# Cross attention and routed FFN on one core: block weights copied to fixed places by SyncE, half of the first normalisation on ScalarE

## The reference

```
c = layernorm(x)
s = (c @ w_c + b_c) + (q @ w_q + b_q)^T + (c * w_cq) @ q^T + b_cq      # 1024 x 6404
a = softmax(s over q);  c2q = a @ q
b = softmax(max(s over q) over c);  q2c = b @ c
x1 = x + concat(c, c2q, c * c2q, c * q2c) @ W_l^T + b_l
x2 = layernorm(x1)
e = argmax(x2 @ wr + br)                                               # one of 8 experts per row
out = x1 + gelu(x2 @ w1[e] + b1[e]) @ w2[e] + b2[e]                    # 128 -> 512 -> 128
```

## Time and profile before

| | us |
|---|---|
| runs, median of 3 (lowest, highest) | 248.47 (247.41, 249.51) |
| the profiled execution: its own time | 250.54 |
| its span, first to last instruction | 248.8 |
| busy: TensorE / VectorE / ScalarE / GpSimd | 205.6 / 184.9 / 161.8 / 138.6 |
| TensorE clock, mean of the span | 0.947 of full |

### The profile page before, as it was taken

One profiled execution on the slowest core, in us unless ns is written; L12 is line 12 of the kernel. 1 busy time (PEld: TensorE's weight loads), 2 busy tenths in 40 slices (PEclk: granted clock), 3 DMA queues, 4 the chain that ended last, 5 costly groups with the idle time before them and its releaser, 6 DMA issues.

```text
span 248.8 us, 5155 instructions
## 1 busy us (share of the span) xinstructions
PE 205.6 (83%) x1833; PEld 151.3 (61%) x1833; DVE 184.9 (74%) x403; ACT 161.8 (65%) x251; POOL 138.6 (56%) x187
## 2 busy tenths in 40 slices
PE   0348699579999999999999998999819747999980
PEld 0114263446776776767767767899719636888860
DVE  1897889767798998998989989589673524555660
ACT  2369579689479699699796996893133513665530
POOL 2449999896952915979429977440027100044443
PEclk9999997979999999999999999999955977999997
DMA  6997989999999999999999999799102550000000
GB/s 214 394 345 232 346 224 229 259 245 146 213 258 163 261 206 231 256 208 229 189 262 236 200 212 204 167 194 234 32 3 103 163 179 0 14 14 29 30 12 0
DMA packets 126951, 44.39 MB, mean 178 GB/s; under 512 B 107720, under 2 KB 124765, under 8 KB 126926
## 3 DMA queue, kind: packets, MB, share of 16 engines
q1 hardware_dynamic: 125992, 42.68, 76.3%
q0 software_dynamic: 784, 1.38, 1.7%
q10 hardware_dynamic: 150, 0.00, 0.0%
HBM read 14.02 MB, written 3.75 MB: 71 GB/s over the span
## 4 chain that ended last, share of the span: by engine, by line
PE 60%; DVE 21%; issue 8%; DMA 5%; ACT 2%; another core or an unknown queue 1%; POOL 1%; DVEq 0%; ACTq 0%; POOLq 0%
PE psX L972 8%; PE psS L957 7%; PE psS L959 7%; PE psO L972 7%; PE psS L958 7%; DMA PT<-Phl 4%; PE psX L975 4%; PE psO L975 4%; DVE Phl L741 3%; PE psS L1172 3%; DVE S L724 3%; DVE c_sb L685 2%; PE psS L1157 2%; DMA S<-in_x 2%; PE psS L1159 2%
## 5 line engine op out<-in xcount | busy, mean ns | idle before, releaser
L587 ACT ACTIVATE S<-S,negb 128x1024 f32<-128x1024 f32 x48 | 55.0, 1145 | 20.5 <-DVE negb L732 20.5
L724 DVE TENSOR_SCALAR_CACHE_REDUCE S<-psS 128x1024 f32<-128x1024 f32 x48 | 58.4, 1216 | 12.2 <-PE psS L959 12.1
L741 DVE TENSOR_TENSOR Phl<-S,Phl 128x1024 f16<-128x1024 f32 x40 | 51.6, 1291 | 5.4 <-ACT Phl L602 5.4
L602 ACT CAST Phl<-S 128x1024 f16<-128x1024 f32 x48 | 50.2, 1045 | 5.1 <-DMA PT<-Phl 3.7
L957 PE MATMUL psS<-qTh,gh 128*128 128x512 f16 (+1 forms) x104 | 41.0, 394 | 9.7 <-DVE qTl L710 5.6
L472 POOL TENSOR_TENSOR Phl<-S,Phl 128x256 f16<-128x256 f32 x32 | 21.9, 715 | 37.0 <-ACT Phl L602 37.0
L959 PE MATMUL psS<-qTh,gl 128*128 128x512 f16 (+1 forms) x104 | 40.8, 392 | 0.0
L958 PE MATMUL psS<-qTl,gh 128*128 128x512 f16 (+1 forms) x104 | 40.8, 392 | 0.0
L972 PE MATMUL psO<-qn,PT 128*128 128x256 f16 x204 | 37.5, 278 | 2.5 <-DMA PT<-Phl 2.5
L972 PE MATMUL psX<-qn,PT 128*128 128x256 f16 x204 | 36.4, 273 | 0.7 <-DMA PT<-Phl 0.7
L975 PE MATMUL psO<-qn,PT 128*128 128x128 f16 x204 | 36.0, 222 | 0.0
(11 more groups left out here) (196 smaller groups left out, 420.3 us busy)
## 6 DMA issues: line engine op xcount, KB each, us to landing
stageT<-in_ctxT SPq DMA_DIRECT2D x6, 512.0 KB, 7.1
PT<-in_ctx SPq DMA_DIRECT2D x6, 512.0 KB, 6.6
w2p<-in_w SPq DMA_DIRECT2D x4, 512.0 KB, 7.3
stageT<-in_w SPq DMA_DIRECT2D x4, 512.0 KB, 6.2
rows_by_expert<-stageT SPq DMA_DIRECT2D x4, 385.5 KB, 4.0
S<-rows_by_expert SPq DMA_DIRECT2D x2, 514.0 KB, 6.1
S<-rows_by_expert SPq DMA_DIRECT2D x2, 385.5 KB, 5.2
PT<-Phl SPq DMA_TRANSPOSE x48, 4.0
```

What stands on the lines that cost most here:

```text
L587: nc.scalar.activation(slot(t, e), slot(t, e), ACT.Exp, bias=negb[:, t:t + 1], accum_out=Lp[:, t * NG + e:t * NG + e + 1]).then_inc(exp_do ...
L602: nc.scalar.copy(hi, slot(t, e)).then_inc(high_done, 1)
L724: nc.vector.tensor_scalar(out=into, in0=bank(u, n)[:, 0:into.shape[1]], scalar1=1.0 / GS, scalar2=None, op0=ALU.mult, op1=ALU.max, accum_o ...
L741: nc.vector.tensor_tensor(lo, slot(t, e), hi, ALU.subtract).then_inc(low_done, 1)
```

## The change

1. `w1p` and `w2p` become the two halves of one tile `wp` (4 x 4096 f16 per partition). SyncE, not TensorE, loads the 14 experts into registers, right behind the last transpose (waiting for the weights' split, `w_low`, and for `experts_ready`), and copies each dispatched block's weights (4 x 512 f16 per partition, 512 KB over the partitions) from `wp` to one of 12 fixed places in the rooms of `PT` and `qn`, which attention no longer needs. The first four copies stand ahead of SyncE's wait for the scattered rows, the other ten behind the four reads of `rows`; the last two reuse a place and wait for an earlier block's `down`. The copy of the last tile's result to `out` now stands behind all of them.
2. `up` and `down` use fixed addresses. The one-hot row of a dispatched block is a column of a new small tile `chosen`, read with step 0; VectorE makes it with two small instructions behind `bexp`, GpSimd a constant `row_no` for it with two more.
3. At the start VectorE makes group 1 of `qTl` ahead of the statistics of tiles 4 to 7, and the rest of the normalisation's small steps among the first scores; the four tile-wide instructions go to ScalarE (Identity with scale `rstd` and bias -mean x `rstd`), behind `qTh` and ahead of `qn`. ScalarE's square root for them moves from ahead of group 2 of `qTh` to ahead of group 4. TensorE transposes these tiles (`turn_c(1)`) after group 3 instead of group 1.
4. VectorE's low parts of the last tile's groups 5 and 6 stand ahead of `residual(0)` and its statistics. GpSimd makes the low part of tile 1, group 3 ahead of the one-hot constants (3 instructions) instead of behind them.

The core of the diff:

```diff
+            expert_reg = [sp.alloc_register(f"expert{j}") for j in range(NB)]
+            sp.wait_ge(w_low, T)
+            sp.wait_ge(experts_ready, 1)
+            sp.reg_load(expert_reg, bexp[0:1, :])
+            ex = [sp.snap(r, min_val=0, max_val=E - 1) for r in expert_reg]
+            def fetch(b):
+                if b >= WSLOTS:
+                    sp.wait_ge(y_in_psum, E + b - WSLOTS + 1)
+                sp.dma_start(block_w(b), wp[:, :, bass.ds(ex[b] * F, F)]).then_inc(block_w_landed[b % WSLOTS], 16)
+            for b in range(FIRST):
+                fetch(b)
             sp.wait_ge(rows_sent, 16 * TA)
             for g, (s0, s1) in enumerate(BATCHES):
                 sp.dma_start(rows[:, s0:s1, :],
                              xs[s0 * P:s1 * P, :].rearrange("(b p) w -> p b w", p=P)).then_inc(rows_landed[g], 16)
+            for b in range(FIRST, NB):
+                fetch(b)
@@ ScalarE
-                if n == 2:
+                if n == 4:
                     deviation(2, H, T)
...
+            act.wait_ge(shift_ready, 1)
+            for t in range(H, T):
+                nc.scalar.activation(c_sb[:, t, :], x_sb[:, t, :], ACT.Identity, bias=sc1[:, t:t + 1],
+                                     scale=rstd[:, t:t + 1]).then_inc(c_late_ready, 1)
@@ VectorE
-            for n in range(NG):
-                if n in DVE_LOW:
-                    low_qT(n)
-                if n >= 1:
-                    scores(0, n - 1)
+            low_qT(1)
+            statistics(x_sb, H, T)
+            variance(H, T)
+            scores(0, 0)
+            low_qT(3)
+            deviation(H, T)
+            nc.vector.scalar_tensor_tensor(out=sc1[:, H:T], in0=mv[:, H:T, 0], scalar=-1.0, in1=rstd[:, H:T],
+                                           op0=ALU.mult, op1=ALU.mult).then_inc(shift_ready, 1)
+            scores(0, 1)
+            low_qT(4)
+            scores(0, 2)
+            scores(0, 3)
+            low_qT(6)
+            scores(0, 4)
+            scores(0, 5)
...
+            low(T - 1, 5)
+            low(T - 1, 6)
             residual(0)
             statistics(x1, 0, H)
-            low(T - 1, 5)
-            low(T - 1, 6)
...
+            dve.wait_ge(route_consts, ROUTE_CONSTS)
+            link(nc.vector.tensor_scalar(bexpf[:, :], bexpf[:, :], float(E - 1), None, ALU.min))
+            nc.vector.tensor_scalar(chosen[:, :], bexpf[:, :], row_no[:, :], None, ALU.is_equal).then_inc(chosen_rows, 1)
@@ TensorE
-                if c == 3:
+                if c == 7:
                     turn_c(1)
...
+                    pe.wait_ge(block_w_landed[j % WSLOTS], 16 * (j // WSLOTS + 1))
+                    pe.wait_ge(chosen_rows, 1)
...
-                if b == E - 4:
-                    pe.wait_ge(experts_ready, 1)
-                    pe.reg_load(expert_reg, bexp[0:1, :])
-                    ex = [pe.snap(r, min_val=0, max_val=E - 1) for r in expert_reg]
```

More of the change, by code:

```diff
@@ L274, in build @@
         rows_landed = [sem(f"rows_landed{g}") for g in range(len(BATCHES))]
+        block_w_landed = [sem(f"block_w_landed{k}") for k in range(WSLOTS)]
+        chosen_rows = sem("chosen_rows")
         xT_in_psum = sem("xT_in_psum")
@@ L670, in statistics, with variance, deviation @@
                 link(last)
[L672 removed]
+            def variance(t0, t1):
                 r = slice(t0, t1)
                 nc.vector.tensor_scalar(sc2[:, r], mv[:, r, 1], EPS, None, ALU.add).then_inc(var_ready, 1)
+            def deviation(t0, t1):
+                r = slice(t0, t1)
                 norms[0] += 1
@@ L1134, in turn, with weights, bias_rows @@
                 last.then_inc(xT_in_psum, 1)
-            expert_reg = [pe.alloc_register(f"expert{j}") for j in range(NB)]
-            def where(first, size):
-                return slice(first, first + size) if isinstance(first, int) else bass.ds(first, size)
+            def weights(b):
+                return wp[:, :, b * F:(b + 1) * F] if b < E else block_w(b - E)
+            def bias_rows(b):
+                return pick[:, b, :] if b < E else chosen[:, b - E:b - E + 1].broadcast_to([P, P])
             def up(b):
@@ L1155, in up @@
                     dst = psH[i][:, f * P:(f + 1) * P]
-                    w_h, w_l = (w1p[:, a, where(e * F + f * P, P)] for a in range(2))
+                    w_h, w_l = (weights(b)[:, a, f * P:(f + 1) * P] for a in range(2))
                     nc.tensor.matmul(dst, w_h, xTp[:, 0, j, :], start=True, stop=False)
@@ L1160, in up @@
                     last = nc.tensor.matmul(dst, b12[:, f * P:(f + 1) * P],
-                                            pick[:, where(e, 1), :].rearrange("p o w -> p (o w)"),
-                                            start=False, stop=True)
+                                            bias_rows(b), start=False, stop=True)
                 last.then_inc(h_in_psum, 1)
             def down(b):
-                i, e = b % RING, ex[b - E] if b >= E else b
+                i = b % RING
                 if b >= RING:
```

43 lines of the change are left out of this document (29 added, 14 removed).

## The result

The changed kernel takes **241.67 us** (median of 5: 238.71, 240.14, 241.67, 245.92, 247.31), the kernel before beside it 248.47; ratio 0.967, 95% interval 0.961 to 0.973.

A forecast was written before the change was run, and what follows sets the result against it. TensorE was taken to bound the middle, with losses at the start and in the experts. A 6.2 + B 4.2 + C 2.9 + D 0.5 = 13.8 us off the median 248.47 gave 234.7 us, range 231.5 to 240.

The forecast's parts named there:

- A: Experts, between down(3) and up(8): no register load on TensorE and no low clock behind it, 6.2 us.
- It fits by 1.4 us: Experts: batch 0 of `rows` lands at about 201.5, needed by 202.9, despite four copies ahead.
- B: Experts, up(8) to up(21): fixed addresses bring dispatched blocks to 22.4 us instead of 26.60, 4.2 us.
- Rival 4: Experts: register instructions aren't the pace of dispatched blocks, B is 0.5 and the time 238.4 us; chance 0.08.
- rivals 1 and 3: Copies bind at 224 GB/s, 239.6 us (chance 0.15); copies don't overlap, 262.8 us at 4.0 a copy (chance 0.04).
- C: Start: the new order starts tile 0's exponential and tile 2 earlier, 2.9 us, bounds 0 and 3.9.
- D: The other orders: last transposes start 2.2 us earlier, waits of 0.70 and 0.2 us go, 0.5 us.
- From there it is always busy: Start: VectorE works without a wait from 19.4, so tile 0's `negb` comes at about 29.
- Group 3 of `qTl`, small steps to 19.4: Start: VectorE finishes these by 19.4, ScalarE gets the shift at 19.5 and starts the exponential at 30.5 instead of 32.86.
- The transposes may start at 34.7, behind drained loads: Start: w2 loads go out 5.8 us earlier, so ScalarE's 2.56 us and VectorE's 1.67 us waits go.
- I count 1.0 us for a longer stretch at 1.2 GHz: Before tile 2: TensorE idles some 4 us instead of 1.99, then about 5 us of low clock instead of 3.3.
- Rival 2: Start: its gain is lost, C falls to 0.5 and the time is 237.1 us; chance 0.17.

The follow-up runs named there:

- e3: The changed kernel run again, unaltered, for a second profile: 241.39 us, ratio 0.967; the profiled execution took 241.56 us.
- e8: Kernel before with the new start alone, GpSimd making `gl` early and pausing before `qn` group 3 until VectorE's first low part: 247.59 us, ratio 0.993.
- e6: e1 without any weight copies or register load, dispatched blocks using fixed experts' weights (output not the reference's): 240.31 us, ratio 0.961.
- e9: e1 with two weight copies instead of four ahead of the reads of `rows`: 239.08 us, ratio 0.963.
- e5: e1 with the reads of `rows` ahead of all weight copies: 240.74 us, ratio 0.965.
- e13: Kernel before with TensorE's register load kept, register addresses only in the last block (output not the reference's): 242.75 us, ratio 0.984.
- second group: The slower seven of the changed kernel's fifteen executions, over several chips: 245.7 to 249.2 us.
- e11: e10 with VectorE's small steps and the shift ahead of group 3 of `qTl`: 237.20 us, ratio 0.955.
- e14: e11 with the four w2 loads issued behind tile 0's transposes instead of ahead of them: 238.11 us, ratio 0.964.
- e10: Changed kernel with GpSimd making `gl` early and pausing until VectorE's first low part, and two copies ahead of the reads: 237.29 us, ratio 0.955.
- e17: The kernel of e11 once more, on another chip: 237.95 us, ratio 0.957.
- e16: e14 with one w2 load behind the transposes of each of tiles 0 to 3, not all four behind tile 0's: 240.98 us, ratio 0.969.
- first group: The faster eight of the changed kernel's fifteen executions, over several chips: 238.3 to 241.7 us.
- e1: Changed kernel with the start and other orders put back as before, leaving SyncE's copies and the fixed addresses: 240.21 us, ratio 0.962.
- e2: Kernel before with the new start alone: 254.67 us, ratio 1.023.

## Why the prediction was wrong

Five of its steps failed: losses of one execution were taken from the median, batch 0 of `rows` came late, VectorE's first low part was taken as free of GpSimd, ScalarE's exponential and the first transposes came no sooner, and the clock cost more than the 1.0 us set for it.

**The sum.** The 13.8 us were read off an execution of 250.54 us and taken from the median, 248.47. From the profiled execution the forecast was 236.7, and e3, the nearest in kind, has 241.56: 4.9 us of the 7.0 are terms, and 2.1 are this step. That such a profile holds losses which the median hasn't is shown for A (block 5 to 8 takes 10.79 us in e8 with the same instructions).

**A, 6.2 us: right in its mechanism, short on one step.** Hole and clock loss went; without lateness of the rows, block 5 to 8 takes 6.77 us (e6, e9), better than the 7.2 worked out. The step that failed is "It fits by 1.4 us". Batch 0 came 0.97 us late. SyncE's load took 3.82 us in e3's trace, near the 3.5 assumed (`bexp` at 186, first copy at 190.4). But the reads were issued 13.05 us after the first scatter, 10.7 before and 10.8 in e5, which has the reads first: the scatter lands later among the copies, and 2.1 MB stand ahead of the reads. (In e9 it is still 12.91 us, but with two copies ahead batch 0 is in time.) Of this the prediction had said only that a late batch 0 was possible, among the "other small things" at 0.06. The granted clock behind that wait was 0.57, between its levels of 1.2 and 2.4 GHz, and block 8 to 9 took 2.84 us instead of 2.05 (before, and in e9). In e3's trace that is 1.3 us of A and 0.8 of the 1.4 that B lacks.

**B, 4.2 us: right in kind.** 4.0 us by e13. The likeliest pace, 1.72 us a block with the transposes in it, isn't reached: 1.83 in e3, 1.75 in e9, 1.81 in e6 without copies; 2.05 before. Single late blocks are 1.61 apart (209.10 to 210.71). Rival 4 is out.

**The copies: right.** At 348 to 386 GB/s, not 224, and overlapped: rivals 1 and 3 are out. Behind 218 us the DMA share falls, as the 220.3 for the last copy says.

**C, 2.9 us: wrong, and the worst of the terms.** With D it is 2.1 us short in e3 and 6 more in the second group. Four steps of C:
- "From there it is always busy": VectorE's first low part, 6 us longer in about half of all executions. Neither the range nor a rival had it. The profile of before had the material: 26 GpSimd subtractions in an unbroken row beside that instruction, which itself took 1.75 us, not the 1.22 of the next. The prediction gave neither a term.
- "Group 3 of `qTl`, small steps to 19.4": the steps took 0.59 instead of 0.16 us beside GpSimd's group 5, the shift came at 21.3, and ScalarE's exponential at 32.8; 0.6 of this is the Identities' price. Shown by e11, which gets 31.1.
- "The transposes may start at 34.7, behind drained loads": with the new start and the loads ahead they start at 38.0 us or later (38.58 in e3), and at 34.43 in e14. The loads issued earlier take 6.8 to 9.1 us to issue instead of 4.12. When they start the queue isn't empty: in the changed kernel the DMA share is 1.05 from 26 to 30, in the kernel before it was 0.23 from 30 to 32.
- "I count 1.0 us for a longer stretch at 1.2 GHz": with tile 2 at 46.84, as the forecast had it (e14), the low clock costs 2.5 us (5.08 against 2.61 to group 1). In e3, which starts tile 2 at 49.89, it costs 1.7, and it costs as much in the kernel before (51.03 to 55.32).

"A microsecond that its stream starts earlier comes out at the end" was right as far as the traces show: from group 1 of tile 2 to `negb` of tile 7 it is 97.3 to 97.8 us in e3, e10, e11 and e17. It fails where loads are moved into that stretch (e16).

Rival 2, the start's gain lost, was right in kind at 0.17. In the first group the new start isn't worth anything that the times show (e3 ratio 0.967, e1, without it, 0.962, intervals overlapping); in the second it costs 6 us. With the GpSimd moves it gains 1.8 us (e10 beside e9).

**D, 0.5 us: nothing.** `negb` of tile 7 to the first scatter takes 31.95 us before (152.87 to 184.82) and 31.92 in e3 (151.58 to 183.50); in e1, with the old orders, 31.97.

The forecast's terms against e3: 10.4 for A and B, 7.8 came; 3.4 for C and D, 1.3 came; and then the second group. A version better than both kernels is e11's, 237.2 and 237.95 us on two chips: 1.9 us under e9, which has the old start, on one chip, and 7.8 us under the change's median on the other.

## What to carry over

Where an instruction with two SBUF inputs on VectorE is moved, list what GpSimd runs then: an unbroken stream can hold it off to the stream's end, in some executions and not in others, and a pause in the stream costs little if what is queued behind the stream is taken out first. Before counting an earlier start, ask what TensorE will wait for behind it: here longer waits were followed by stretches at half clock, which took back 1.7 to 2.5 us. A profile is one execution: compare its time with the median before its losses are taken from the median. Register addresses and a register load on TensorE are worth taking off a hot path: 4 us and 3 to 5 us here, and no cost of 7 MB of copies behind the work was seen, within 2 us.

## What the runs showed of the hardware

- A 128 x 1024 subtraction on VectorE took 1.22 us at the median, or 7.5 us beside 26 of GpSimd's subtractions; then it ended 1.1 us after GpSimd's last. In those executions GpSimd's 26 took 16.34 us and none over 0.86; where VectorE got in they took 20.4 to 22.4 us and the longest 1.69. Which of the two comes about, in the same program, stays open: e2 in its profile and, by their times, in all four executions, the change in 7 of 15 executions by their times, the kernel before in its profile not.
- 128 x 4 steps on VectorE: 0.16 us alone, 0.59 beside GpSimd's 128 x 256 subtractions.
- TensorE's granted clock was 0.50 for 3 to 6 us behind waits of 2.80 us (e3), 3.65 (e11) and 4.34 (e14), and stayed at 1.00 behind waits of 2.56 (e10) and 3.53 (e8). The length of the last wait doesn't tell the two apart.
- Copies from SBUF to SBUF with a register address: 348 to 386 GB/s, and SyncE issues four in 4.27 us.
- A load of 14 registers takes 3.82 us on SyncE and 3.54 on TensorE (e3, before). TensorE's idle time for it was 3.25 us in e13, where only a single one of them is used.
